# Four heads a step in the 16-head layers, and one row of products in the layer over leading positions

## What is computed

```python
# causal: 16 heads of width 8, batches of 256 positions
scores = einsum('bhqd,bhkd->bhqk', q, k) / sqrt(8) + triu_mask
out = einsum('bhqk,bhkd->bhqd', softmax(scores), v) @ Wo.T
# binary: the same without the mask; q, k, v, out by binarised weights with biases
Wb = mean(abs(W), axis=1) * sign(W)
# lead: the leading axis is the sequence (8 keys), the 256 positions are the batch, 16 heads of width 8
scores = einsum('sbhd,tbhd->bhst', q, k) * 8 ** -0.5
out = einsum('bhst,tbhd->sbhd', softmax(scores), v)
```

## Time and profile before

| | us |
|---|---|
| median of 3 runs (4507.86 to 4510.74) | 4509.04 |
| the profiled execution | 4513.09 |
| its span in the trace | 4511.3 |
| PE, DVE, ACT, POOL busy | 4027.8, 2763.2, 2729.5, 3001.0 |

### The profile page before, as it was taken

How to read it: one execution, slowest core, us unless ns; L and a number is a source line. 1 busy time by engine, 2 the same in 40 slices (tenths; PEclk the granted TensorE clock), 3 DMA queues, 4 the chain that set the end, 5 groups by cost and what they waited for, 6 DMA issues and landing times.

```text
span 4511.3 us, 169577 instructions
## 1 busy us (share of the span) xinstructions
PE 4027.8 (89%) x69543; PEld 2810.5 (62%) x69543; DVE 2763.2 (61%) x4602; ACT 2729.5 (61%) x5657; POOL 3001.0 (67%) x1858
## 2 busy tenths in 40 slices
PE   8979999999999999977999999999999995367975
PEld 5656666666666666635666666666666663154654
DVE  4556666666766667635667666676666663524541
ACT  5656676666766766635667667576675763134652
POOL 0068888888888888816888878788787882421011
PEclk9999999999999999989999999999999997587987
DMA  2023343434334343312334333343333330040004
GB/s 68 2 59 94 101 104 91 108 92 105 100 92 111 90 103 101 96 30 60 94 102 103 94 101 95 101 103 94 101 96 99 102 90 19 0 119 8 1 11 124
DMA packets 349841, 368.13 MB, mean 82 GB/s; under 512 B 58738, under 2 KB 285171, under 8 KB 348787
## 3 DMA queue, kind: packets, MB, share of 16 engines
q1 hardware_dynamic: 338834, 348.79, 30.0%
q0 software_dynamic: 2048, 4.20, 0.3%
q10 hardware_dynamic: 8160, 3.93, 0.3%
HBM read 246.99 MB, written 109.71 MB: 79 GB/s over the span
## 4 chain that ended last, share of the span: by engine, by line
PE 42%; ACT 2%; POOL 2%; DVE 2%; issue 2%; DMA 1%; DVEq 0%; POOLq 0%; ACTq 0%
PE banks L328 7%; PE banks L359 4%; PE banks L407 4%; PE banks L333 3%; PE banks L451 3%; PE banks L312 3%; PE banks L295 2%; PE banks L879 2%; PE banks L377 2%; PE banks L897 1%; PE banks L445 1%; PE banks L914 1%; PE banks L392 1%; PE banks L1345 1%; PE banks L1365 1%
## 5 line engine op out<-in xcount | busy, mean ns | idle before, releaser
L671 POOL TENSOR_TENSOR arena<-arena 128x512 f32<-128x512 f32 x768 | 960.0, 1271 | 461.3 <-DVE arena L600 266.5
L676 POOL TENSOR_TENSOR arena<-arena 128x1024 f32<-128x1024 f32 x384 | 905.9, 2359 | 30.1
L673 POOL TENSOR_TENSOR arena<-arena 128x1024 f32<-128x1024 f32 x384 | 908.1, 2365 | 0.0
L600 DVE SCALAR_TENSOR_TENSOR arena<-arena,banks 128x512 f32<-128x512 f32 x768 | 493.6, 684 | 537.3 <-ACT arena L500 528.7
L328 PE MATMUL banks<-w_qk,arena 128*128 128x512 f32 x1536 | 734.8, 601 | 16.0 <-DVE arena L700 10.6
L461 ACT COPY arena<-banks 128x512 f32<-128x512 f32 x384 | 224.6, 585 | 660.0 <-PE banks L407 660.0
L593 DVE TENSOR_REDUCE arena<-arena 128x8 f32<-128x512 f32 x768 | 494.0, 679 | 83.4 <-ACT arena L477 81.0
L477 ACT ACTIVATE arena<-banks 128x512 f32<-128x512 f32 x768 | 441.7, 594 | 62.0 <-PE banks L328 49.4
L407 PE MATMUL banks<-ident,arena 128*128 128x128 f32 x3072 | 427.1, 282 | 34.9 <-POOL arena L676 22.8
L328 PEld LDWEIGHTS banks<-w_qk,arena 128*128 128x128 f32 x1536 | 277.0, 193 | 272.1 <-issue 272.0
L333 PEld LDWEIGHTS banks<-w_v,arena 128*128 128x128 f32 x1536 | 293.9, 191 | 206.6 <-issue 186.5
(11 more groups left out here) (220 smaller groups left out, 6744.8 us busy)
## 6 DMA issues: line engine op xcount, KB each, us to landing
v_rows<-arena SPq DMA_DIRECT2D x1536, 64.0 KB
arena<-v_rows SPq DMA_DIRECT2D x768, 128.0 KB
arena<-v_rows SPq DMA_DIRECT2D x768, 112.0 KB
arena<-in_moe_w SPq DMA_DIRECT2D x30, 515.5 KB, 3.8
w_qk<-in_stack_qk SPq DMA_DIRECT2D x48, 256.0 KB, 3.0
w_v<-in_stack_v SPq DMA_DIRECT2D x48, 128.0 KB, 3.2
w_o<-in_stack_o SPq DMA_DIRECT2D x12, 512.0 KB
w_w<-in_stack_w SPq DMA_DIRECT2D x12, 341.0 KB, 3.0
```

Of the source, the lines that this page charges most:

```text
L600: last = nc.vector.scalar_tensor_tensor(qn[:, :, tile], rn, 1e12, bank(M, tile).rearrange("p (h q d) -> p h q d", h=GH, q=2), ALU.min, ALU ...
L671: nc.gpsimd.tensor_tensor(f.sined[:, :, :, half, :], x[:, :, :, 1 - half, :], sines[:, :, mine].unsqueeze(1).to_broadcast([D, GH, 4, DH // ...
L673: nc.gpsimd.tensor_tensor(rot, x.rearrange("p h t a d -> p h t (a d)"), cosines.unsqueeze(1).to_broadcast([D, GH, 4, DH]), ALU.mult).then_ ...
L676: nc.gpsimd.tensor_tensor(rot, rot, f.sined.rearrange("p h t a d -> p h t (a d)"), ALU.add).then_inc(S.rotated, 1)
```

## The change

In the 16-head layers a `Quad` takes the place of two pairs: four heads' scores go to banks 0 to 3, one bank a row group. Causal scores lie close together, 128 columns of the first row tile and 256 of the second, and the mask product covers only the two diagonal blocks, written as two runs of 128 columns. The probabilities are turned in two halves, one ahead of the next quad's scores and one behind them. Each head's values and ones stand at its own 8 of 32 columns, the rest being zeros, so that a batch's four quads accumulate in bank 6 and are normalised once; the output weights need no padding and one product. Maxima are taken by head and row tile. The layer's q, k and v projections are queued behind the value products. In the lead layer qkv, scores, probabilities and results exist once a tile, and the products have four buffers; POOL issues the 16 score products and then the 16 value products. Lines that only go away are left out below, since the functions stand above.

```diff
 def causal_mask():
-    q = np.arange(T).reshape(2, 128).T[:, :, None]
-    return np.where(np.arange(T)[None, None, :] > q, np.float32(NEG), np.float32(0)).reshape(D, 2 * T)
+    return np.tile(np.triu(np.full((D, D), NEG, np.float32), 1), (1, 4))
...
+    f = arena(M, dict(q=(T,), k=(2, T), qm=(2, 4, T), vs=(2, 8, 160), os=(160,), p=(2, 4, 2, T), pt=(2, 4, 2 * T),
+                      ntop=(2, 4, 2), lg=(T,), inv=(T,), ot=(T,), wraw=(4, D), sgn=(D,), neg=(D,), wsum=(4,), wt=(4, D)))
+    v = f.vs[:, :, :, 0:128].rearrange("p a g (c e) -> p a g c e", c=4)
+    v_in = f.vs.rearrange("p a g (c e) -> p a g c e", c=4)[:, :, :, :, 0:8]
+    ones = f.os[:, 0:128].rearrange("p (c e) -> p c e", c=4)
+    return namedtuple("Heads", f._fields + ("v", "v_in", "ones"))(*f, v, v_in, ones)
...
+class Quad:
+    def __init__(self, m, n):
+        self.n, self.b, self.c = n, n // 4, n % 4
+        self.width = 384 if m.causal else 512
+        self.keys = (slice(0, 128), slice(128, 384)) if m.causal else (slice(0, T), slice(T, 2 * T))
...
+    def project_out(b):
+        pe.wait_ge(S.divided, b + 1)
+        pe.wait_ge(S.v, min(b + 3, B))
+        pe.matmul(bank(M, 7, T), w.o, f.ot, start=True, stop=True).then_inc(S.out_projected, 1)
...
+    def turn(h, half):
+        pe.wait_ge(S.probs, 2 * h.n + half + 1)
+        if h.n or half:
+            pe.wait_ge(S.copied_first, 2 * h.n + half)
+            pe.wait_ge(S.copied_second, 2 * h.n + half)
+        for i in range(2):
+            o = 0
+            for kt in range(2):
+                for qt in range(kt if m.causal else 0, 2):
+                    last = pe.transpose(bank(M, 4 + i)[:, o:o + 128],
+                                        f.p[:, h.n % 2, 2 * half + i, qt, kt * 128:kt * 128 + 128], M.ident[:])
+                    o += 128
+        last.then_inc(S.turned, 1)
+    for n in range(QUADS + 3):
+        if 0 <= n - 1 < QUADS:
+            turn(Quad(m, n - 1), 0)
+        if n < QUADS:
+            h = Quad(m, n)
+            if h.c == 0:
                 pe.wait_ge(S.k, h.b + 1)
                 pe.wait_ge(S.q_masked, h.b + 1)
+            if n >= 1:
+                pe.wait_ge(S.probs, 2 * n)
             if m.causal:
+                for j in range(4):
+                    pe.matmul(bank(M, j).rearrange("p (t k) -> p t k", t=2)[:, :, 0:128], M.identb[:],
+                              M.cmask[:, 0:2 * 128], start=True, stop=False, skip_group_check=True)
             for t in range(2):
+                cols = h.keys[t]
+                for j in range(4):
                     r = slice(32 * j, 32 * j + 32)
+                    last = pe.matmul(bank(M, j)[:, cols], f.qm[r, h.b % 2, h.c, t * 128:t * 128 + 128],
+                                     f.k[r, h.b % 2, 0:cols.stop - cols.start], start=not m.causal, stop=True,
+                                     skip_group_check=m.causal)
             last.then_inc(S.scores, 1)
...
+        if 0 <= n - 1 < QUADS:
+            turn(Quad(m, n - 1), 1)
+        if 0 <= n - 2 < QUADS:
+            h = Quad(m, n - 2)
+            pe.wait_ge(S.copied_first, 2 * h.n + 2)
+            pe.wait_ge(S.copied_second, 2 * h.n + 2)
             pe.wait_ge(S.v, h.b + 1)
+            if h.c == 0 and h.b >= 1:
+                pe.wait_ge(S.divided, h.b)
             for o in (0, T):
                 for kt in range(2):
                     q0 = 128 * kt if m.causal else 0
                     for j in range(4):
+                        val = f.v[:, h.b % 2, 4 * kt + j, h.c, :] if o == 0 else f.ones[:, h.c, :]
                         last = pe.matmul(bank(M, 6)[32 * j:32 * j + 32, o + q0:o + T], val,
+                                         f.pt[:, h.n % 2, j, kt * T:kt * T + T - q0],
+                                         start=(h.c == 0 and o == 0 and kt == 0), stop=(h.c == 3 and kt == 1),
+                                         skip_group_check=True)
             last.then_inc(S.pv, 1)
+        if n % 4 == 0 and n // 4 + 1 < B:
+            project_qk(n // 4 + 1)
+        if n % 4 == 1 and n // 4 + 1 < B:
+            project_v(n // 4 + 1)
+        if n % 4 == 2 and n >= 6:
+            project_out(n // 4 - 1)
...
+    def copy(h, half):
+        act.wait_ge(S.turned, 2 * h.n + half + 1)
+        if h.n >= 2:
+            act.wait_ge(S.pv, h.n - 1)
+        nc.scalar.copy(f.pt[:, h.n % 2, 2 * half, 0:h.width], bank(M, 4, h.width)).then_inc(S.copied_first, 1)
+    def exponentials(h, half):
+        if h.n >= 2:
+            act.wait_ge(S.turned, 2 * h.n - 2)
+        for j in (2 * half, 2 * half + 1):
+            act.wait_ge(S.maxed, 4 * h.n + j + 1)
+            for t in range(2):
+                cols = h.keys[t]
+                last = nc.scalar.activation(f.p[:, h.n % 2, j, t, 0:cols.stop - cols.start], bank(M, j)[:, cols],
+                                            ACT.Exp, bias=f.ntop[:, h.n % 2, j, t:t + 1])
+        last.then_inc(S.probs, 1)
+    def invert(b):
+        act.wait_ge(S.pv, 4 * b + 4)
+        nc.scalar.activation(f.lg, bank(M, 6)[:, T:2 * T], ACT.Ln).then_inc(S.logged, 1)
+        act.wait_ge(S.logged, b + 1)
+        if b >= 1:
+            act.wait_ge(S.divided, b)
+        nc.scalar.activation(f.inv, f.lg, ACT.Exp, scale=-1.0).then_inc(S.inverted, 1)
+    for n in range(QUADS + 3):
+        if 0 <= n - 1 < QUADS:
+            copy(Quad(m, n - 1), 0)
+        if n < QUADS:
+            exponentials(Quad(m, n), 0)
+        if 0 <= n - 1 < QUADS:
+            copy(Quad(m, n - 1), 1)
+        if n < QUADS:
+            exponentials(Quad(m, n), 1)
+        if n % 4 == 1 and n >= 5:
+            invert(n // 4 - 1)
+        if n % 4 == 0 and n // 4 + 1 < B:
+            take_qk(n // 4 + 1)
+        if n % 4 == 1 and n // 4 + 1 < B:
+            take_v(n // 4 + 1)
...
+    nc.vector.memset(os[:, :, 8:40], 0.0)
+    nc.vector.memset(os[:, :, 0:8], 1.0).then_inc(S.zeroed, 1)
...
+    def copy(h, half):
+        dve.wait_ge(S.turned, 2 * h.n + half + 1)
+        if h.n >= 2:
+            dve.wait_ge(S.pv, h.n - 1)
+        nc.vector.tensor_copy(f.pt[:, h.n % 2, 2 * half + 1, 0:h.width],
+                              bank(M, 5, h.width)).then_inc(S.copied_second, 1)
+    def maxima(h, half):
+        dve.wait_ge(S.scores, h.n + 1)
+        for j in (2 * half, 2 * half + 1):
+            for t in range(2):
+                last = nc.vector.tensor_reduce(f.ntop[:, h.n % 2, j, t:t + 1], bank(M, j)[:, h.keys[t]], AX.X, ALU.max,
+                                               negate=True)
+            last.then_inc(S.maxed, 1)
+    for n in range(QUADS + 3):
+        if 0 <= n - 1 < QUADS:
+            copy(Quad(m, n - 1), 0)
+        if n < QUADS:
+            maxima(Quad(m, n), 0)
+        if 0 <= n - 1 < QUADS:
+            copy(Quad(m, n - 1), 1)
+        if n < QUADS:
+            maxima(Quad(m, n), 1)
+        if n % 4 == 1 and n >= 5:
+            b = n // 4 - 1
+            dve.wait_ge(S.inverted, b + 1)
+            if b >= 1:
+                dve.wait_ge(S.out_projected, b)
+            nc.vector.tensor_tensor(f.ot, bank(M, 6)[:, 0:T], f.inv, ALU.mult).then_inc(S.divided, 1)
+        if n % 4 == 2 and n >= 6:
+            residual(n // 4 - 1)
...
+    return arena(M, dict(qkv=(2, B, 3 * D), prod=(4, B * D), sc=(2, B, B, 16), pr=(2, B, B, 16), top=(B, 16),
+                         tot=(B, 16), inv=(B, 16), att=(2, B, D), at=(4 * D,)))
...
+    for j in range(2 * B):
+        if j >= 4:
+            pe.wait_ge(S.qkv, j - 3)
+        o = j % B * T + j // B * 128
+        pe.matmul(bank(M, j % 4, 3 * D), M.z[:, o:o + 128], w.qkv, start=True, stop=True).then_inc(S.projected, 1)
+    for i in range(4):
+        t, half = i // 2, i % 2
+        pe.wait_ge(S.att, t * B + 4 * half + 4)
+        for s in range(4):
+            last = pe.transpose(bank(M, 4 + i % 2)[:, s * D:s * D + D], f.att[:, t, 4 * half + s, :], M.ident[:])
+        last.then_inc(S.turned, 1)
+        pe.wait_ge(S.at, i + 1)
+        if i >= 2:
+            pe.wait_ge(S.residual, i - 1)
+        pe.matmul(bank(M, 6 + i % 2), w.o, f.at, start=True, stop=True).then_inc(S.out_projected, 1)
...
+    for j in range(2 * B):
+        act.wait_ge(S.projected, j + 1)
+        nc.scalar.copy(f.qkv[:, j // B, j % B, :], bank(M, j % 4, 3 * D)).then_inc(S.qkv, 1)
...
+        sc, pr = f.sc[:, t], f.pr[:, t]
...
+    for t in range(2):
         for s in range(B):
+            j = (2 + t) * B + s
             dve.wait_ge(S.prod, j + 1)
+            nc.vector.tensor_reduce(f.att[:, t, s, :], f.prod[:, j % 4, :].rearrange("p (t c) -> p c t", t=B),
                                     AX.X, ALU.add).then_inc(S.att, 1)
...
+    for j in range(4 * B):
+        t, s = j // B % 2, j % B
+        if j >= 4:
+            if j - 4 < 2 * B:
+                pool.wait_ge(S.reduced, j - 3)
+            else:
+                pool.wait_ge(S.att, j - 3 - 2 * B)
+        qkv = f.qkv[:, t]
+        if j < 2 * B:
+            pool.wait_ge(S.qkv, (t + 1) * B)
```

(7 more changed lines are left out.)

251 lines of the change are left out of this document (38 added, 213 removed).

## The result

The changed kernel takes **4407.07 us** (median of 4 runs, 4402.87 to 4410.59) against 4509.27 of the kernel before on the same chip: a ratio of 0.9774, 95% interval 0.9759 to 0.9789. That is 102.2 us less where 89.9 was forecast. The profiled execution took 4402.87, its span 4401.1.

What follows compares the result with a forecast made beforehand. TensorE was taken to bound both 16-head layers, GpSimd products, softmax and reductions the lead layer; 37.3 + 37.3 + 15.3 = 89.9 us, so 4513.1 - 89.9 - 4.0 = 4419 us, range 4400 to 4470.

Steps and rivals of the forecast that it cites:

- Four row groups: 16-head layers: a quad's 16 score passes run four at once, 1.06 us binary and 0.86 causal.
- two wide: Rival, 16-head layers: four row groups don't run at once; 47 us more, 4466 us, chance 10%.
- The ring: 16-head layers: scores, maxima, exponentials, scores again over one bank set; 5.57 us binary, 5.19 causal; batches 23.7 and 20.9.
- Masks, normalisation, output projection: 16-head layers: four masks 0.53 us, one normalisation a batch costs nothing, output projection 0.5 us fits TensorE's wait.
- The cold fronts: Starts of the 16-head layers at granted clock 0.50, rising about when it does now: 4 us causal, 6.4 binary.
- an early clock: Lower end of the range: with an early clock and a lead layer without cost, the kernel takes 4400 us.
- The tails: 16-head layers behind the last scores, up to product and residual: 10.4 us causal, 12.0 binary.
- One sign of being wrong: 16-head layers: a granted clock below 1.00 behind the first 25 us of each would show the forecast wrong.
- The lead layer: Lead layer: GpSimd's 32 products in one row over four buffers, VectorE setting the late pace; 15.3 us less.
- The meetings: Lead layer: two-input VectorE operations meet GpSimd products; 3 us taken, bounds 0 and 8; rival at full 8: 4424, 12%.
- The sum: Whole kernel: 37.3 causal, 37.3 binary and 15.3 lead make 89.9 us less, giving 4419 us.
- the one on small reductions: Rival, 16-head layers: small reductions cost more and VectorE closes the ring; 31 us more, 4450 us, chance 10%.

Runs made afterwards that it cites:

- two_wide_wait: Changed kernel with TensorE waiting for the end of heads 0 and 1's score passes before those of heads 2 and 3 start: 4480.2 us, 0.9930.
- narrow_copy: Changed kernel with ScalarE's copy between the two halves' exponentials cut from 384 or 512 columns to 64, from a layer's third quad on: 4404.6 us, 0.9762.
- pair_maxima: Changed kernel with VectorE's maxima reductions put together for two heads (one in the binary layer, two in the causal), signalled at the end: 4436.3 us, 0.9838.
- three_logs: Changed kernel with ScalarE taking the logarithm of a batch's sums three times instead of once in both 16-head layers: 4418.4 us, 0.9784.
- combo2: The kernel of combo without the 12 filler products ahead of the causal layer: 4396.2 us, 0.9749.
- lead_psum: Changed kernel with the lead layer's maxima and reciprocals kept in two free PSUM banks instead of SBUF: 4407.4 us, 0.9775.
- two_wide: Changed kernel with a quad's 16 score passes issued pair by pair, heads 0 and 1 before heads 2 and 3: 4408.8 us, 0.9782.
- twelve_more: Changed kernel with only 12 unused bf16 products of 512 columns added behind the causal layer's normalisation: 4426.6 us, 0.9818.
- combo: Changed kernel with lead residual moved, lead maxima and reciprocals in PSUM, one binary reduction per head, filler products around three layers' starts: 4419.7 us, 0.9791.

## Why the prediction was right, and where it wasn't

**Four row groups** (1.06 and 0.86 us a quad): 1.08 and 0.87 from start to start. Right, and shown: two_wide_wait. The rival's price was too low: 47 us for "two wide" against 70, for its rings grew by 1.0 and 1.2 us, not 0.67 and 0.85; about 0.2 of that is the experiment's own wait (2.33 us for two pairs of 1.06), so 57 without it.

**The ring.** Binary batch 23.7 forecast, 23.90 measured; single rings 5.57, 5.92 and 6.66 against 5.63 to 5.72, 5.90 and 6.65. Causal batch 20.9 against 21.36: the rings with a projection take 5.30 instead of 5.19 to 5.32, the plain one 5.37 and 5.55 in turn (why in turn is open). The mis-sized terms are the latencies between engines: the first exponential comes 0.78 us behind the scores, not 0.71, and TensorE goes on 0.15 behind the last probabilities, not 0.03. 31 rings of 5.34 are 165.6 us instead of 161.8; the binary layer's are 184.2 instead of 182.7. Which engine closes them was half right: ScalarE does, but VectorE is so close behind that a shorter copy gave only 0.07 us a ring in the causal and 0.01 in the binary layer (narrow_copy), and the order "first head first" is worth 26 us in the two layers (pair_maxima).

**Masks, normalisation, output projection**: 0.54 for 0.53; the normalisation nothing for nothing, with nothing to spare (three_logs), but for the last binary ring, 6.23 us instead of 5.63, and 6.78 in three_logs (it has no v projection ahead of it, in whose ring the logarithm and exponential hide elsewhere; that this is why is not shown); the output projection 0.54 from start to start for 0.5.

**The cold fronts** (the low clock at both layers' starts) were the step that failed, by 11 us: 4 and 6.4 us were charged for them, and the runs show none over steady rings. I had the clock rise when it does now; it rose 5.4 us earlier in the causal layer (33.60 against 38.97) and 6.2 us behind the first maxima in the binary one, not 19.4. From the first maxima to the last scores' end the layers took 164.7 and 184.1 us, no more than 31 steady rings (165.6 and 184.2). TensorE in the binary layer, behind the first maxima:
```profile
4044.76 2.08 PE L846 MATMUL banks<-z,arena 128*128 128x256 f32 x4
4047.32 1.97 PE L879 MATMUL banks<-ident,arena 128*128 128x128 f32 x8 [0.49 <-ACT arena L977]
4049.22 2.05 PE L904 MATMUL banks<-arena 32*128 32x256 f32 x16
```
The three take 1.13, 1.04 and 1.15 us at 1.00, so the low clock gave TensorE 2.8 us more work by then. Part of that the ring's waits hid: from the first maxima to the start of the third scores it is 10.8 us, and 9.3 in combo2, where the clock is at 1.00 (some 0.1 of it by another edit). So the low clock cost some 1.4 us. Two steady rings with the same projections would need 11.3 us at 1.00: the first two, which have no values to multiply yet (1.87 us each in TensorE), give back some 1.9, and the last ring takes 0.6 more than a steady one. I had 6.4 us for the one and nothing for the other; an early clock stood only behind the lower end of my range. The longer rings took back 5.3 of the 11. So the causal layer came out right by luck, because two errors cancelled: 175.05 us (32.35 to 207.40) for 176.2. The binary one took 196.4 for 201.1, and 2.1 us less ahead of the first maxima, 1.3 of them in the normalisation's first products (5.40 us instead of 6.67), where the clock happened to stand otherwise. The tails were 10.4 and 12.3 us for 10.4 and 12.0. One sign of being wrong did show: the binary layer's clock was below 1.00 until 38.4 us behind its start, where I had named 25. It was a bad sign, since it already stood so in the kernel before (53.8 us).

**The lead layer**: 15.7 us less for 15.3, but by other terms. The meetings cost VectorE 1.27, 0.36 and 0.50 us (2.1 for the 3 taken), and lead_psum shows that they are meetings; the upper bound was too high because VectorE waits only for the rest of a product. The 16 last reductions run 1.81 us apart (14.55 and 14.46 for eight), not 1.92: in the kernel before each also waited for a product. That gave 18.3 us behind the first product. And 2.6 went back ahead of it (22.6 us from the layer's start, 20.05 before), where the clock was at 0.50 for longer. That isn't the change's: of the ten variants without fillers ahead of this layer, six have 20.0 to 20.5 us there and four 22.7 to 22.9, like the changed kernel.

**The sum.** Layers 98.8 us with 0.5 of the shorter start, for 89.9; the rest of the 102.2 is in the unchanged layers and in the spread of the runs. The forecast came out right with the largest gain, four row groups, priced rightly, and with the fronts' error partly cancelled by the rings'. None of the rivals held; the one on small reductions adds up to 28 us by its own rings, not 31. What the single normalisation, the one output product and the narrower masks gave is read from rows alone: no run undoes them one by one. The clock stayed at 1.00 in both layers with TensorE at 92 to 96%.

## What to carry to other kernels

Where a few row groups of the array are used, look at what four of them in flight would give: the second pair of heads was free. A ring over one set of banks is priced by the latencies in it (first small result, hand-over), and a term of 0.1 us counts 62 times. After an edit compare the stages that weren't edited as well: they can take back more than a layer gave.

## What the runs showed of the hardware

- Row groups don't keep the program's order among them. In two_wide four passes start within 0.04 us and all sixteen in four such groups, 0.2 to 0.3 us apart, though the first eight are written for heads 0 and 1 alone; in two_wide_wait, where a wait holds heads 2 and 3 back, they come two at a time. A row doesn't name its head, so that heads 2 and 3 ran ahead of passes written before them is read from this count; what sets the order isn't shown.
- Unchanged code got slower by instructions ahead of it: the two stacks together took 3468.7 to 3477.6 us in the changed kernel and ten of its variants, 3478.9 in the kernel before, and 3495.4 and 3502.5 in the two with 12 more matmuls ahead of the first stack. TensorE's busy time is within 0.5% of the same. The clock isn't behind it in twelve_more: its stacks ran 116.0 us at 0.50, the changed kernel's 117.2 (combo's 131.1). Nor is it one place: against combo2, matmul by matmul, twelve_more's first stack is 5 us late at its half and 14 at its end. That the position of the instructions is behind it is a guess; another number than 12 wasn't tried.
- VectorE's 1024-element product with two inputs in SBUF takes 1.23 us alone and 1.58 to 2.50 beside a GpSimd product; with one input in PSUM it is 1.22 and GpSimd isn't held either. "SBUF — State Buffer" of the Trainium skill, "Who interferes with whom", has it so; but a meeting cost VectorE 0.4 to 1.3 us, well below a whole product of 2.3, since it waits for the rest of the one under way.
- Stages that nobody edited come in two lengths, by where the clock stood. The single layer takes 68.8 to 68.9 us in nine of the fourteen traces, where a stretch of 10.2 us at 0.50 ends 23.4 to 24.3 us into it, and 72.4 to 72.7 in the other five (combo2 among them), where the stretch is 17.1 us long and ends at 30. The lead layer's front differs by 2.5 us in the same manner. A difference of 3 or 4 us between two medians is therefore no evidence here without the stages.
